# Multiplying the heads' outputs by their row factors on GpSimd instead of VectorE, each piece behind a mask of the decays

## The reference, cut to what matters

```python
def step(state, xs):
    q_t, k_t, v_t, g_t, b_t = xs
    state = state * jnp.exp(g_t)[..., None, None]
    kv = jnp.einsum('bhk,bhkv->bhv', k_t, state)
    delta = (v_t - kv) * b_t[..., None]
    state = state + jnp.einsum('bhk,bhv->bhkv', k_t, delta)
    out = jnp.einsum('bhk,bhkv->bhv', q_t, state)
    return (state, out)
...
o = o * jax.nn.silu(z.astype(jnp.float32))
o = o * jax.lax.rsqrt(jnp.mean(o * o, axis=-1, keepdims=True) + EPS)
o = o * norm_gamma
...
return o @ w_out
```

## Time and profile before

| what | value |
|---|---|
| median of 3 runs | 1712.46 us (1711.25 to 1715.58) |
| the profiled execution | 1705.38 us |
| its span | 1703.5 us |
| TensorE busy with products | 1492.6 us, 88% of the span |
| VectorE busy | 1019.7 us, 60% |
| ScalarE busy | 767.5 us, 45% |
| GpSimd busy | 875.0 us, 51% |
| mean granted TensorE clock | 0.946 of full speed |

### The profile page before, as it was taken

One profiled execution on the slowest core, in us unless ns is written; L12 is line 12 of the kernel. 1 busy time (PEld: TensorE's weight loads), 2 busy tenths in 40 slices (PEclk: granted clock), 3 DMA queues, 4 the chain that ended last, 5 costly groups with the idle time before them and its releaser, 6 DMA issues. The chain is left out here.

```text
span 1703.5 us, 26260 instructions
## 1 busy us (share of the span) xinstructions
PE 1492.6 (88%) x9462; PEld 1077.1 (63%) x9462; DVE 1019.7 (60%) x2090; ACT 767.5 (45%) x1748; POOL 875.0 (51%) x1304
## 2 busy tenths in 40 slices
PE   2646999999999999999999999999769789689884
PEld 2324777787777777877777777777545445455553
DVE  2435777777767777677777776775530455451443
ACT  0322655656556556565565664654421245210111
POOL 0076676566665675666657666570100178315343
PEclk9677999999999999999999999999989899979997
DMA  8111111111111111101111111100052100012676
GB/s 203 44 31 35 36 26 36 34 38 35 22 39 32 35 35 35 38 23 32 41 29 38 35 28 36 32 20 13 7 228 96 31 1 1 30 51 78 132 146 144
DMA packets 126384, 86.25 MB, mean 51 GB/s; under 512 B 92146, under 2 KB 112454, under 8 KB 125488
## 3 DMA queue, kind: packets, MB, share of 16 engines
q1 hardware_dynamic: 120112, 76.04, 16.1%
q0 software_dynamic: 6144, 8.53, 3.0%
HBM read 61.45 MB, written 23.49 MB: 50 GB/s over the span
## 5 line engine op out<-in xcount | busy, mean ns | idle before, releaser
L580 PE MATMUL psum_banks<-main_hT,heads_w_in 128*128 128x512 f32 x512 | 248.1, 611 | 19.0 <-DVE heads_y L882 11.0
L882 DVE SCALAR_TENSOR_TENSOR heads_y<-psum_banks,gdn_conv_w,heads_y 128x1021 f32<-128x1021 f32 (+2 forms) x192 | 244.6, 1275 | 27.6 <-ACT heads_y L756 26.7
L1069 POOL TENSOR_TENSOR heads_XT<-heads_XT,heads_tmp 128x126 f32<-128x126 f32 (+22 forms) x496 | 207.4, 418 | 38.9
L1066 POOL TENSOR_TENSOR heads_tmp<-heads_XT,heads_A 128x126 f32<-128x126 f32 (+22 forms) x496 | 183.6, 370 | 38.9
L1405 POOL TENSOR_SCALAR attn_prob<-attn_prob,attn_rtotal 128x1024 f32<-128x1024 f32 x32 | 90.6, 2844 | 144.6 <-DVE attn_rtotal L1372 144.6
L580 PEld LDWEIGHTS psum_banks<-main_hT,heads_w_in 128*128 128x128 f32 x512 | 93.6, 195 | 94.3 <-issue 68.9
L667 PE MATMUL psum_banks<-heads_w_z,main_hT 128*128 128x256 f32 x512 | 126.8, 392 | 0.0
L756 ACT ACTIVATE heads_y<-psum_banks,gdn_conv_w 128x1024 f32<-128x1024 f32 x64 | 71.3, 1113 | 113.1 <-PE psum_banks L580 113.1
L693 PE MATMUL psum_banks<-heads_w_o,heads_ogT 128*128 128x256 f32 x512 | 119.2, 382 | 2.9 <-ACT heads_ogT L818 1.0
L778 ACT ACTIVATE heads_Dt<-heads_Dl,gdn_coef 128x128 f32<-128x128 f32 x224 | 77.3, 393 | 90.8 <-DVE heads_Dl L895 89.5
L1053 POOL TENSOR_TENSOR heads_Dm<-heads_Dm,main_upto 128x512 f32<-128x512 f32 x64 | 87.0, 1380 | 52.4 <-ACT heads_Dm L816 52.4
(11 more groups left out here) (243 smaller groups left out, 3416.5 us busy)
## 6 DMA issues: line engine op xcount, KB each, us to landing
main_w_gu<-in_w_gu SPq DMA_DIRECT2D x4, 2816.0 KB, 22.8
heads_w_in<-in_w_in SPq DMA_DIRECT2D x16, 512.0 KB, 3.5
heads_A<-kk_blocks SPq DMA_DIRECT2D x64, 128.0 KB
moe_wd<-in_w_down SPq DMA_DIRECT2D x32, 176.0 KB
expert_rows<-main_zeros SPq DMA_DIRECT2D x1, 4624.0 KB, 24.9
moe_be<-expert_rows SPq DMA_DIRECT2D x32, 144.5 KB, 3.2
heads_w_z<-in_w_z SPq DMA_DIRECT2D x16, 256.0 KB, 2.7
heads_w_o<-in_w_o SPq DMA_DIRECT2D x16, 256.0 KB, 2.6
```

What stands on the lines that cost most here:

```text
L580: ins = pe.matmul(out[:, half * 512:(half + 1) * 512], w_in[:, kd_, j * P:(j + 1) * P], hT[:, kd_, half * 512:(half + 1) * 512], start=kd_ ...
L882: dve.scalar_tensor_tensor(y[j][:, shift:T], src[:, 0:T - shift], conv_w[:, head, j, t:t + 1], y[j][:, shift:T], ALU.mult, ALU.add).then_i ...
L1066: pool.tensor_tensor(tmp[:, 0:n, 0:m], bc_last(XT[:, 0:n, j], m), bc_mid(A0[:, j, j + 1:BLK], n), ALU.mult).then_inc(solve_step.sem, 1)
L1069: pool.tensor_tensor(XT[:, 0:n, j + 1:BLK], XT[:, 0:n, j + 1:BLK], tmp[:, 0:n, 0:m], ALU.add).then_inc(solve_step.sem, 1)
```

## The change

VectorE no longer multiplies `og` by `fac` at the places 6, 8, 9 and 11. GpSimd does it, with the same operation and the same four pieces, each right behind the mask of the decays with the same number. `fac` itself stays on VectorE. The pieces get a semaphore of their own, `normed`, on which the transposes `flip0` to `flip3` wait.

```diff
 AT = {"variance": 3, "factors": 6, "turn": 8, "scales": 13, "keys": 5, "key_squares": 8}
-NORMALIZE = [6, 8, 9, 11]
...
-    tail_dve = Uses(a.sem("tail_vector"), ["rqs", "rq2", "var0", "var", "fac", "ogn0", "ogn1", "ogn2", "ogn3"], FINISH)
+    tail_dve = Uses(a.sem("tail_vector"), ["rqs", "rq2", "var0", "var", "fac"], FINISH)
+    normed = Uses(a.sem("outputs_normalised"), ["0", "1", "2", "3"], FINISH)
...
                 elif name.startswith("flip"):
-                    pe.wait_ge(tail_dve.sem, tail_dve.done(h, f"ogn{u}"))
+                    pe.wait_ge(normed.sem, normed.done(h, str(u)))
...
-            def normalize(h, u):
-                if u == 0:
-                    dve.wait_ge(tail_dve.sem, tail_dve.done(h, "fac"))
-                mine = og[h % 2][:, 4 * u:4 * u + 4]
-                dve.tensor_tensor(mine, mine, bc_last(fac[:, 4 * u:4 * u + 4], P), ALU.mult).then_inc(tail_dve.sem, 1)
...
-                        if k in NORMALIZE:
-                            normalize(h, NORMALIZE.index(k))
...
+            def normalize(h, u):
+                if u == 0:
+                    pool.wait_ge(tail_dve.sem, tail_dve.done(h, "fac"))
+                mine = og[h % 2][:, 4 * u:4 * u + 4]
+                pool.tensor_tensor(mine, mine, bc_last(fac[:, 4 * u:4 * u + 4], P), ALU.mult).then_inc(normed.sem, 1)
...
-                if h in INVERT:
-                    for g in range(4):
-                        mask_decay(h, g)
+                for u in range(4):
+                    if h in INVERT:
+                        mask_decay(h, u)
+                    if h in FINISH:
+                        normalize(h, u)
```

## The result

The changed kernel took 1697.29 us as a median of 4 runs (1695.87 to 1698.30); the kernel before, in 4 runs beside it, 1712.13 us (1711.25 to 1715.58). The ratio is 0.9909, with a 95% interval of 0.9892 to 0.9926: 12.7 to 18.5 us faster. Foretold were 1701 us, 11.5 us less than before, so the direction was right and the size too small. The profiled execution took 1698.25 us. In all sets disturbed executions are left out of the ratios; there was one, of 8394 us, of the kernel before beside e13 to e16.

A forecast was written before the change was run, and what follows sets the result against it. The prediction took TensorE as the bound, with pauses at L705. Its terms, -9.1 - 1.1 - 3.2 + 0.5 + 1.4 = -11.5 us, took the median from 1712.46 to 1701 us, range 1697 to 1710.

The forecast's parts named there:

- slower: Rival: in each step VectorE's L921 waits for GpSimd's whole run, making p4 late; +52 us, 1764 us, chance 0.1.
- given back at `p4`: Rival: L921 loses nearly a full GpSimd instruction each step, so the tap delays p4; -1.8 us, 1711 us, chance 0.2.
- The clock term of step 15: Behind TensorE's wait for Dl in step 15: a shorter pause leaves the clock up, -3.2 us (0 to -3.2).
- the term of the 13 steps: Steps 2 to 14: L705 starts up to 0.88 us earlier, taken as 0.7 a step, -9.1 us (-2.6 to -11.4).
- Step 15, -1.1 us foretold: TensorE's wait for Dl in step 15 shortens without the first piece ahead of the transposes: -1.1 us (0 to -1.4).
- the clock falls more often in the steps: Sign of being wrong: TensorE's clock falls more often in the steps because it no longer pauses; no size given.
- Steps 16 and 17, +1.9 us foretold: Last steps: L921 falls among GpSimd's pieces in step 16, +0.5 us; slower pieces delay step 17's transposes, +1.4 us.

The follow-up runs named there:

- e13: The kernel before, unchanged, run against itself on another chip than e9: 1705.58 us against 1706.98, ratio 0.9994.
- e16: The kernel before with all four pieces still on VectorE, at places 6, 9, 11 and 12: 1692.94 us, ratio 0.9933.
- e7: The changed kernel with each piece multiplied three times on GpSimd, twice into a spare tile: 1707.05 us, ratio 0.9992.
- e1: The kernel before with all pieces still on VectorE, pieces 1 to 3 moved to places 11, 12 and 12: 1693.72 us against 1709.49, ratio 0.9910.
- e4: The changed kernel with piece 1 of step 15 alone back on VectorE, ahead of the transposes: 1697.17 us, ratio 0.9928.
- e9: The kernel before, unchanged, profiled a second time: 1720.02 us, with 1721.74 for the kernel before beside it.
- e10: The kernel before, unchanged, profiled a third time: 1721.40 us, with 1721.74 for the kernel before beside it.
- e14: The changed kernel, measured again on another chip than e9: 1697.13 us, ratio 0.9944.
- e3: The kernel before with only piece 2 (place 9) moved to GpSimd: 1701.36 us, ratio 0.9952.
- e2: The kernel before with only piece 1 (place 8) moved to GpSimd: 1694.54 us, ratio 0.9915.
- e12: The same kernel as e2, profiled once more: 1713.39 us, with 1721.74 for the kernel before beside it.
- e15: The same kernel as e1, run on the same chip as the changed kernel: 1695.21 us against 1706.98, ratio 0.9938.

## Why the prediction fell short

**What held.** In the steps 2 to 14 the two pieces of places 8 and 9 were on the path of TensorE, and those of 6 and 11 weren't. L705's wait for `v_s` is gone and one for `kneg` stands there. The transposes, `Dl`, `Dt` and `kneg` moved as the working says. GpSimd had the room. Neither slower nor "given back at `p4`" came true.

**What failed.** Two steps of the sum. The clock term of step 15 (-3.2 us) had the mechanism wrong: neither does the wait always bring the clock down, nor did the clock give anything in all. And the term of the 13 steps had the mechanism right and the size too small, because it charged a collision that fits into slack. The first erred towards too much gain, the second towards too little, so that the total came out as close as it did is in part luck.

**The 13 steps, -9.1 us foretold, -11.4 measured.** Undisturbed steps fell from 68.7 to 67.8 us, which is the full 0.88 us that the prediction had worked out for L705 and then lowered to 0.7. It lowered it for a collision at L921, with a piece of 1.25 us on GpSimd. The piece takes 1.05 us, like the columns and not like the masks, so the lists stand otherwise; L921 took 0.73 us in place of 0.51, the tap ends at 672.20 and `p4` follows at 672.40, without a wait. The slack is in the prediction's own figures: without a collision the tap ends at 674.06, and TensorE can't use it before 674.51, 0.10 of which `p4` needs behind it, so 0.35 us are free. The collision cost 0.31 (0.73 less its median of 0.42). The prediction should have taken the two cases apart, the collision that fits into the slack and the one that doesn't, in place of a middle between them.

The Trainium skill (SBUF — State Buffer, "SBUF: two separate sides") says that VectorE and GpSimd exclude each other on a shared port pair for a whole instruction, when VectorE has two SBUF inputs (and GpSimd reads SBUF) or is in a mode that uses both port pairs. The runs agree for two inputs: L921, which has them, takes 0.42 to 1.16 us in the changed kernel by where it falls. In e7 the `TENSOR_SCALAR` of 128x32, with one input, took 1.02 us against 0.18 in e1; no run shows in which mode it ran.

**Step 15, -1.1 us foretold, -1.7 measured.** The wait for `Dl` went away as a whole, and e4, which brings 1.27 us of it back, pays 1.8 us. TensorE after, step 15, for the earlier trace rows:

```profile
1139.60 0.71 PE L615 MATMUL psum_banks<-heads_Dl,heads_At 128*128 128x128 f32 x4
```

By the table, where the clock stayed up from step 14 to 15, it is 63.0 us (e9, e10) against 61.3 (e14). Foretold was only the length of the piece of place 8 beside GpSimd. The prediction held that the piece of place 6 lies on no path, since no row shows a wait behind it; in this step it does. It made the next L921 late, at 1142.60 us just behind the first mask (1142.43), so that L921 took 1.38 us; in the changed kernel L921 comes at 1135.24, ahead of the mask at 1135.46, and takes 0.42. The waits of 1.61, 1.27 and 0.46 us named under e4 show both shares.

**The clock, -3.2 us foretold, about 0 measured.** It made the fall in step 15 a consequence of the 1.61 us wait. But all four profiles of before have that wait, and the clock fell in two of them; e3 and e4 have it (1.61 and 1.27 us) and the clock stayed up. Where it falls it costs 2.8 us, so on average there were 1.4 us to gain here, if the change ends these falls; three profiles of after without one don't show that for certain. One fall of another kind came on top. TensorE after, around 883 us:

```profile
878.00:883.00 5.00, 5.00 (x27) 3.35 (x25) 0.78 (x3) 2.56 (x6) 0.76 (x1) 1.00 0.40 107
883.00:888.00 5.00, 5.00 (x116) 4.56 (x116) 3.53 (x10) 2.98 (x10) 3.09 (x2) 0.72 0.01 3
```

TensorE is busy throughout, ahead of it too, and at 0.72 over these 5 us it ran a part of them, from 885 us on, at the lower of its two levels, 1.2 GHz. A step with such a fall takes 69.2 us in place of 67.8, so a fall costs 1.43 us. From step 2 to 15 there are three in the kernel before and four after: +1.4 us. The prediction had named "the clock falls more often in the steps" among what would make it wrong, and gave it no term.

**Steps 16 and 17, +1.9 us foretold, +1.1 measured** (86.9 against 85.8 us). Rows of step 16, in order of time, then of step 17:

```profile
1185.29 4.22 POOL L1051 TENSOR_TENSOR heads_og<-heads_og,heads_fac 128x512 f32<-128x512 f32 x4 [1.90 <-DVE heads_fac L949]
1187.63 0.98 DVE L921 TENSOR_TENSOR heads_og<-heads_og,heads_z 128x256 f32<-128x256 f32 x1
1189.19 0.71 PE L609 MATMUL psum_banks<-heads_X,heads_Uf 128*128 128x128 f32 x4 [0.74 <-DVE heads_X L890]
```

```profile
1221.91 4.04 POOL L1051 TENSOR_TENSOR heads_og<-heads_og,heads_fac 128x512 f32<-128x512 f32 x4 [0.29 <-DVE heads_fac L949]
1223.00 3.88 PE L687 MATMUL psum_banks<-main_ident,heads_og 128*128 128x128 f32 x16 [5.79 <-POOL heads_og L1051]
1226.15 1.46 ACT L818 ACTIVATE heads_ogT<-psum_banks,gdn_gamma 128x512 f32<-128x512 f32 x2 [0.31 <-PE psum_banks L687]
```

Both mechanisms are there: L921 runs 0.55 us longer in step 16 than in the earlier trace rows, and in step 17 the transposes follow GpSimd's pieces. With 1.05 us a piece this costs 1.1 us in all in place of 1.9. The Trainium skill (GPSIMD Engine Reference, "Elementwise — side-by-side cycle accounting") gives a ratio of 1.96 between the engines, for an addition of 2048 elements; the piece, a multiplication of 512 elements a partition with one repeated operand, has 1.05 / 0.68 = 1.5 here.

**The sum.** -11.4 - 1.7 + 1.1 = -12.0 us for the moved work. The clock adds about -1.4 (step 15, on average) and +1.4 (one more fall), and e13 has one fall more in its first column, another -0.4 in the mean of before. That makes -12.4 against the -12.7 of the stage. The ratio of the first set, 0.9909, means -15.6 us, that of e14, 0.9944, -9.6; their mean, -12.6, is what the stage shows. So the stage explains 12.4 to 12.7 us, and the rest of the first set's 15.6 is the spread of whole runs. In the profiles the times outside the stage differ by over 10 us between executions; for the executions without a profile it isn't known where their spread lies, and it isn't explained.

**The falls inside the steps.** Two things that all 18 profiles show. Each of the short falls in the steps 1 to 15 begins 11.4 to 12.9 us behind a step's first L705, right behind the run of 96 products on 32x32 blocks that stands there (most of the 116 products of the row above). So falls are always a whole number of steps apart. And their number goes with the length of an undisturbed step, not with the pause at L705: four, once three, at 67.8 us; none at 68.2 (e2, e7, e12, e16); one at 68.4 (e3); three at 68.7 (before). e7 pauses 0.27 us at L705 like the changed kernel and has none, and the kernel before pauses 0.6 us like e2 and has three.

**What stays open.** Why the length of a step should decide over the falls: no run varies it by itself. What decides in step 15. And the spread of whole runs.

## What to carry to other kernels

Look which of the moved instructions stand ahead of something that the bound engine waits for, and first try to place them elsewhere on their own engine: here that gave the same time as the move to GpSimd, at no cost in the last steps. Where two paths close at one wait, each taken alone gives only part, so price both. A collision costs nothing as long as it fits into the slack behind it: compare the two before charging it. And when a loop's step gets shorter by under 1%, count the falls of the clock before and after: kernels with steps of 68.2 us and no falls ended level with those of 67.8 us and four.

## What was not expected of the hardware

TensorE's clock falls while it is busy throughout: after, at 476, 680, 885 and 1090 us, 205 us or three steps apart; before, at 339, 684 and 1029 us, 345 us or five steps apart. Each fall costs 1.43 us. They come in other steps in other executions of a kernel, always at the same place of the step, and in the same number from step 2 to step 15, except in e1 and e15 (3 and 4). VectorE's collisions with GpSimd also hit small instructions: the `TENSOR_SCALAR` on 128x32 took 1.02 us in e7.
